# Single fp32 products in place of three rounded products of high and low parts

## What is computed

```python
def attention(h):                      # h: (8, 512, 256)
    q, k, v = heads(h @ W_q.T), heads(h @ W_k.T), heads(h @ W_v.T)
    p = softmax(causal(rope(q) @ rope(k).T / 4))
    return merge(p @ v) @ W_o.T

def ffn(h):                            # h: (4096, 256)
    cw = top4_of_top2_groups(sigmoid(h @ gate_w.T), gate_bias)
    y = sum(cw[:, e] * ((silu(h @ Wg[e].T) * (h @ Wu[e].T)) @ Wd[e].T) for e in range(16))
    return h + y + (silu(h @ Ws_g.T) * (h @ Ws_u.T)) @ Ws_d.T

x = x + ln(attention(ln(x)))
out = x + ln(ffn(ln(x)))
```

## Time and profile before

| what | value |
|---|---|
| time, median of 3 runs | 982.29 us (981.41 to 983.65) |
| profiled execution, span from first to last instruction | 1048.8 us (its time outside the span isn't listed) |
| mean granted clock of PE in it | 0.888 of full |
| busy share of the span: PE, PEld | 81%, 59% |
| busy share of the span: DVE, ACT, POOL | 62%, 44%, 41% |
| chain that ended last, by engine | PE 40%, DVE 23%, issue 11%, SPq 8%, DMA 6% |

### The profile page before, as it was taken

The page is one execution under the profiler, slowest core; times in us unless marked ns, Lnnn a source line. Parts: engine busy times, 40 slices in busy tenths (PEclk is TensorE's granted clock), DMA queues, the critical chain, the costliest instruction groups (busy, mean ns, idle before and its releaser), DMA issues.

```text
span 1048.8 us, 20609 instructions
## 1 busy us (share of the span) xinstructions
PE 852.6 (81%) x6580; PEld 615.2 (59%) x6580; DVE 652.3 (62%) x1914; ACT 456.3 (44%) x763; POOL 426.7 (41%) x408
## 2 busy tenths in 40 slices
PE   4569798987987987987987877978977799989955
PEld 3436374664664663664654545757865588867722
DVE  5577658687687687687586674533642233687916
ACT  2115454544544544544543555425433355544410
POOL 3222113135335335335213234374565555664621
PEclk9759898997897897997987998889999999998978
DMA  4685726236336336336395212453545566997783
GB/s 161 147 222 144 216 64 163 75 98 174 98 99 173 99 99 173 98 81 172 98 322 159 85 47 92 144 167 93 166 150 161 161 178 164 383 314 281 247 339 128
DMA packets 89175, 168.72 MB, mean 161 GB/s; under 512 B 14704, under 2 KB 56688, under 8 KB 88816
## 3 DMA queue, kind: packets, MB, share of 16 engines
q1 hardware_dynamic: 75248, 128.85, 42.1%
q0 software_dynamic: 13824, 38.55, 9.9%
HBM read 90.15 MB, written 76.68 MB: 159 GB/s over the span
## 4 chain that ended last, share of the span: by engine, by line
PE 40%; DVE 23%; issue 11%; SPq 8%; DMA 6%; another core or an unknown queue 5%; ACT 4%; POOL 3%; DVEq 0%; ACTq 0%; POOLq 0%
DVE nmax L829 8%; PE ring L1536 6%; PE ring L1314 5%; PE ring L1316 4%; PE ring L1315 4%; PE ring L1392 3%; PE ring L1557 3%; PE ring L1358 2%; SPq L628 2%; PE ring L1383 2%; SPq L629 2%; DMA xg<-sorted_rows 2%; PE ring L1436 2%; PE ring L1522 2%
## 5 line engine op out<-in xcount | busy, mean ns | idle before, releaser
L1244 ACT ACTIVATE prob<-ring 128x1024 f32<-128x1024 f32 (+1 forms) x192 | 167.5, 881 | 215.5 <-PE ring L1383 196.5
L829 DVE TENSOR_REDUCE nmax<-ring 128x2 f32<-128x1024 f32 (+3 forms) x256 | 201.8, 819 | 73.3 <-PE ring L1365 43.6
L736 POOL DMA_INDIRECT expert_rows<-ys,dest x160 | 159.2, 995 | 127.0 <-ACT ys L1198 74.8
L728 POOL DMA_INDIRECT sorted_rows<-xr,idx_all x128 | 130.5, 1019 | 104.8 <-DVE xr L991 71.5
L1536 PE MATMUL ring<-we,xh 128*128 x640 | 160.3, 396 | 0.0
L1536 PEld LDWEIGHTS ring<-we,xh 128*128 128x128 f32 x640 | 121.6, 200 | 14.6
L1054 DVE SCALAR_TENSOR_TENSOR sl<-sl,got,ring 128x128 f32<-128x128 f32 x160 | 48.3, 343 | 109.8 <-ACT sl L1296 62.5
L1358 PE MATMUL ring<-k_st,q_st 48*128 48x512 f32 (+3 forms) x512 | 88.9, 387 | 26.0 <-issue 9.7
L1392 PE MATMUL ring<-prob,v_sb 128*32 128x512 f32 (+3 forms) x1024 | 106.3, 518 | 3.2 <-ACT prob L1244 3.2
L1377 PE MATMUL ring<-maskt_b,halves_b 64*128 64x128 bf16 (+2 forms) x768 | 58.4, 233 | 50.7 <-DVE nmax L829 23.5
L1377 PEld LDWEIGHTS ring<-maskt_b,halves_b 64*128 64x128 bf16 x768 | 22.8, 97 | 125.4 <-issue 56.7
(11 more groups left out here) (203 smaller groups left out, 1650.8 us busy)
## 6 DMA issues: line engine op xcount, KB each, us to landing
xg<-sorted_rows SPq DMA_DIRECT2D x160, 134.0 KB
parts<-part SPq DMA_DIRECT2D x32, 512.0 KB
ykt<-expert_rows SPq DMA_DIRECT2D x14, 1024.0 KB
k_st<-parts SPq DMA_DIRECT2D x64, 128.0 KB
q_st<-parts SPq DMA_DIRECT2D x64, 128.0 KB
we<-w_exp SPq DMA_DIRECT2D x1, 6144.0 KB
sorted_rows<-zeros SPq DMA_DIRECT2D x2, 2144.0 KB, 9.6
sorted_rows<-zeros SPq DMA_DIRECT2D x32, 134.0 KB
```

The costliest lines, as they stand in the source:

```text
L728: pool.indirect_dma_start(out=xs[group_of(s)], out_offset=bass.IndirectOffsetOnAxis(ap=idx_all[:, s, t, k:k + 1], axis=0), in_=xr[:, s % 2 ...
L736: pool.indirect_dma_start(out=yk, out_offset=bass.IndirectOffsetOnAxis(ap=dest[:, j % 8, b:b + 1], axis=0), in_=ys[:, j % NYS, b, :], in_o ...
L829: dve.tensor_reduce(nmax[:, Q % 2, :, pp, qb], slot[:, :, col:col + (qb + 1) * P], AX.X, ALU.max, negate=True).then_inc(s_max, 1)
L1244: act_e.activation(prob[:, u % 2, 2 * half:2 * half + 2, 0:width], slot[:, :, 0:width], ACT.Exp, scale=SCALE).then_inc(s_exp, 1)
```

## The change

Every dense product becomes one matmul on fp32 tiles. ACT's copy out of PSUM stays (into `xt` and `h_t`); the low parts on DVE and POOL, the copy `a_hi`, the steps `GA`, the splits of the weights and the sum of the logit halves go. The weights are loaded straight into `wq` and `w_all`. What waited for a low part now waits for ACT's copy (`s_xt`, `s_at`, `s_ht`), for DVE's `act` (`SD`), or for the sigmoid (`M_BANK` after the logits). `act` is multiplied in place of its copy, so its next writer waits for the `SD` step of the sequence before. The logits have 16 columns. Nothing else of `PLAN` changes its place.

The diff, cut to its core:

```diff
-         ("GU", 0, 28), ("GU", 1, 28.01), ("GA", 0, 28.5), ("GA", 1, 28.9), ("LGA", 28.75), ("LG", 29.1)]
+         ("GU", 0, 28), ("GU", 1, 28.01), ("LGA", 28.75), ("LG", 29.1)]
...
-            "XT": lambda st: (s_xtlo, KD * (st[1] + 1)),
+            "XT": lambda st: (s_xt, KD * (st[1] + 1)),
...
-            "LGA": lambda st: (s_sumlg, st[1] + 1),
+            "LGA": lambda st: (s_score, st[1] + 1),
...
-            def xt_low(s, slot):
-                for k in range(KD):
-                    dve.wait_ge(s_xthi, KD * s + k + 1)
-                    dve.tensor_tensor(xt_lo[:, k, :], slot[:, k, :], xt_hi[:, k, :], ALU.subtract).then_inc(s_xtlo, 1)
...
                     if n:
-                        dve.wait_ge(s_alo, 2 * n - 1 + u)
+                        dve.wait_ge(s_sd, NHALF * n)
                     dve.tensor_tensor(act[:, u, :], silu[:, u, :], ring[RING_SLOT[st]][:, 1, :], ALU.mult).then_inc(s_t, 1)
-                elif kind == "LG":
-                    dve.wait_ge(s_logit, n + 1)
...
                 elif kind == "LG":
-                    act_e.wait_ge(s_sumlg, n + 1)
+                    act_e.wait_ge(s_logit, n + 1)
                     if n:
                         act_e.wait_ge(s_route, ROUTE_STEPS * n)
-                    act_e.activation(r_sc[:, :], r_lg[:, :], ACT.Sigmoid).then_inc(s_score, 1)
+                    act_e.activation(r_sc[:, :], M_BANK[:, 0:NT * E], ACT.Sigmoid).then_inc(s_score, 1)
...
-            def split_product(dst, l_hi, l_lo, r_hi, r_lo, start, stop, **kw):
-                pe.matmul(dst, l_lo, r_hi, start=start, stop=False, **kw)
-                pe.matmul(dst, l_hi, r_lo, start=False, stop=False, **kw)
-                return pe.matmul(dst, l_hi, r_hi, start=False, stop=stop, **kw)
...
                 for k in range(KD):
-                    last = split_product(slot[:, n, :], *weights(col, k, width, m, P), hi[:, k, :], lo[:, k, :],
-                                         k == 0, k == KD - 1)
+                    last = pe.matmul(slot[:, n, :], weights(col, k, width, m, P), rhs[:, k, :], start=k == 0, stop=k == KD - 1)
...
-                    dst = M_BANK[:, t * 2 * E:(t + 1) * 2 * E]
+                    dst = M_BANK[:, t * E:(t + 1) * E]
                     for k in range(KD):
-                        pe.matmul(dst, h_lo[:, k, tok], w_gate[:, k, :, :].rearrange("p c e -> p (c e)"), start=(k == 0), stop=False)
-                        last = pe.matmul(dst, h_hi[:, k, tok], w_gate[:, k, :, :].rearrange("p c e -> p (c e)"), start=False,
-                                         stop=k == KD - 1)
+                        last = pe.matmul(dst, h_t[:, k, tok], weights(C_GATE, k, E, 0, E), start=k == 0, stop=k == KD - 1)
```

More of the change, by code:

```diff
@@ L270, in block_kernel @@
         part = place("part", [P, 2, 2, T], fp32r)
[L271 to L274, removed]
+        xt = place("xt", [P, KD, T])
+        wq = place("wq", [P, C_O])
         rope_t = place("rope_t", [P, 2, T])
@@ L278, in block_kernel @@
         w_low = cursor[0]
[L279 to L284, removed]
+        w_all = place("w_all", [P, C_ALL - C_O])
+        h_t = place("h_t", [P, KD, T])
         pr = place("pr", [P, NT, D])
@@ L287, in block_kernel @@
         z = place("z", [P, NT, D])
-        a_hi = place("a_hi", [P, 2, T], fp32r)
-        a_lo = place("a_lo", [P, 2, T], fp32r)
+        w_high = cursor[0]
+        xr = place("xr", [P, 2, NT, XROW])
         silu = place("silu", [P, 2, T])
@@ L1116, in _ @@
                     norm_rows(n)
[L1117 to L1125, removed]
                 elif kind == "QK":
@@ L1202, in _ @@
                 slot = ring[RING_SLOT[st]] if st in RING_SLOT else None
-                if kind == "LX" and n == 0:
-                    act_e.wait_ge(s_wq, 16)
-                    copy(wq_hi[:, :], stage[:, 0:C_O], s_whi)
-                elif kind == "LNR" and n == 0:
-                    act_e.wait_ge(s_small, 16)
-                    copy(w_hi[:, :], stage[:, C_O:C_GATE], s_whi)
-                    copy(w_gate[:, :, 0, :], stage[:, C_GATE:].rearrange("p (k e) -> p k e", k=KD), s_whi)
-                elif kind == "XT":
+                if kind == "XT":
                     if n:
@@ L1278, in _ @@
                     act_e.activation(silu[:, u, :], slot[:, 0, :], ACT.Silu).then_inc(s_silu, 1)
-                elif kind == "GA":
-                    u = st[2]
-                    act_e.wait_ge(s_t, 2 * n + u + 1)
-                    if n:
-                        act_e.wait_ge(s_sd, NHALF * n)
-                    copy(a_hi[:, u, :], act[:, u, :], s_ahi)
                 elif kind == "BT1":
@@ L1340, in token_product @@
                     for k in range(KD):
-                        last = split_product(slot[:, t // 2, (t % 2) * D:(t % 2 + 1) * D], lhs_hi[:, k, tok], lhs_lo[:, k, tok],
-                                             *weights(col, k, width, m, D), k == 0, k == KD - 1)
+                        last = pe.matmul(slot[:, t // 2, (t % 2) * D:(t % 2 + 1) * D], lhs[:, k, tok],
+                                         weights(col, k, width, m, D), start=k == 0, stop=k == KD - 1)
                     if t % 2:
@@ L1494, in _ @@
                 elif kind in ("LGA", "LG"):
-                    pe.wait_ge(s_htlo, KD * (n + 1))
+                    pe.wait_ge(s_ht, KD * (n + 1))
                     logits_unit(n, int(kind == "LG"))
                 elif kind == "GU":
-                    pe.wait_ge(s_htlo, KD * (n + 1))
+                    pe.wait_ge(s_ht, KD * (n + 1))
                     for gu in range(2):
-                        channel_product(slot, gu, h_hi, h_lo, (C_SG, C_SU)[gu], D, st[2] * P, gu == 1).then_inc(s_gu, 1)
+                        channel_product(slot, gu, h_t, (C_SG, C_SU)[gu], D, st[2] * P).then_inc(s_gu, 1)
                 elif kind == "SD":
-                    pe.wait_ge(s_alo, 2 * n + 2)
-                    token_product(slot, a_hi, a_lo, C_SD, D, 0, s_sd)
+                    pe.wait_ge(s_t, 2 * n + 2)
+                    token_product(slot, act, C_SD, D, 0, s_sd)
                 elif kind == "CNT":
```

75 lines of the change are left out of this document (20 added, 55 removed).

## The result

| | before | after |
|---|---|---|
| time, median (lowest to highest), 4 runs each | 982.97 us (981.41 to 988.89) | 993.53 us (992.85 to 994.70) |
| span of the profiled execution | 1048.8 us, in a second execution 980.4 us | 989.9 us |

The ratio is 1.0097, interval 1.007 to 1.0125: 9.6 us more between the means, 10.6 between the medians.

The account below looks back on a forecast made before the run. Bound: PE's products and the waits for low parts, 336 to 389 us in a middle sequence. Costs of 4.5 less gains of 2.6 give 1.9 us, over 7.5 sequences 14 us: 996 us, 8 in 10 from 974 to 1020 us.

Parts of the forecast that it names:

- Products: On PE: single fp32 products 0.865 us at 512 columns, 0.433 at 256; 4.7 us more a sequence.
- What of it lies on the chain: Middle sequence, 336 to 389 us: 4.5 us of longer products on the chain; `OP`'s 0.6 us covered beside it.
- 0.4 us for the lower clock: Start of `GU` and half of `SD`: a product's excess is twice as long at the lower clock, 0.4 us more.
- What is given back: PE waits behind removed low parts in each sequence go: together 2.6 us.
- `h_lo`: Behind `HT` 0.85 us and ahead of `OP` 0.26 us of PE waits go in each sequence.
- `xt_lo`: At `XT`: PE's 0.64 us wait for a maximum that stands behind `xt_lo` goes.
- `a_hi` with the logit sum: Logits to sigmoid: PE's 0.85 us wait for `prob` goes.
- even start: First two sequences: products mostly at the lower clock; lost `xt_lo` gives back about what they cost more.
- piece without a name: Ahead of `HT`: unnamed 3.68 us stretch taken as unchanged; moving by 2 us a sequence equals the whole forecast.
- DVE's pace: Rival: DVE sets the pace and hides the products, so the change is faster, 968 us; chance 0.16.
- Nothing is given back: Rival: PE's waits for maxima move along with its later score units, 1020 to 1033 us; chance 0.12.
- The clock of a middle sequence: Rival: longer products keep PE at the upper clock over 349.9 to 356.6 us, 971 us; chance 0.05.

Follow-up runs that it names:

- e7: The kernel after with DVE again subtracting `h_lo`, and the slot and PE's products waiting for it: 999.23 us, ratio 1.016.
- e9: The kernel after with DVE again subtracting `xt_lo`, and the slot and first QK product waiting for it: 1001.73 us, ratio 1.0174.
- e10: The kernel after with `a_hi`, `a_lo` and a DVE pass over the logits ahead of the sigmoid put back: 1005.19 us, ratio 1.0224.
- e1: The kernel before, unchanged, profiled a second time: 982.27 us, span 980.4 us.
- e3: The kernel before with single fp32 products (logits as before), every low part still made and waited for: 1015.8 us, ratio 1.0318.
- e2: The kernel after with three rounded products each (two for the logits), a zero tile as low part, no low parts made: 968.97 us, ratio 0.9852.
- e5: The kernel after with V, SD and OP as three rounded products with a zero low part, QK and GU single: 985.31 us, ratio 1.0018.
- e6: The kernel after with QK and GU as three rounded products with a zero low part; V, SD and OP single: 975.62 us, ratio 0.9923.
- e4: The kernel after with one rounded matmul per product, less precise: 912.78 us, ratio 0.9273.
- e8: The kernel after with two rounded products per product, weights split in two parts, less precise: 940.14 us, ratio 0.9557.

## Why the prediction was right, and where only in the sum

- *Products.* Forecast starts of 0.865 and 0.433 us, measured 0.871 and 0.446; PE 35 us busier, measured 31.7. So the price of the earlier trace rows holds: each of the two records of a product takes about twice as long as a rounded one of its width (0.436 against 0.227 us at 512 columns), the product nearly four times as long. The Trainium skill, Perfetto Trace Analysis, Engine Utilization, halves the rate for FP32_LOW_HIGH; the trace agrees with that for a record, not for a whole product. The logits, taken as nothing, are nothing: four products in 1.00 us, eight rounded records before in 0.99 (337.65 to 338.64 us).
- *What of it lies on the chain.* 4.5 us a sequence (5.1 with `OP`). With the low parts still there it is 4.9 (73.4 to 78.3), of the 5.1 us that the measured starts make, so in sum almost nothing was covered. Without them it is 2.0 (71.8 to 73.8). The forecast took a price read in the trace of before, where it holds, and added it in the kernel after, where it doesn't. Its 0.4 us for the lower clock belong to the odd execution: in the second one the same place has a granted clock of 1.00 (the last but two of the numbers).

```profile
340.50:347.00 6.50, 4.52 (x55) 3.40 (x54) 5.51 (x20) 3.27 (x5) 4.80 (x6) 1.00 0.39 123
```

- *What is given back.* 2.6 us a sequence. With triples 1.6 come back (73.4 to 71.8), with single products 4.5 (78.3 to 73.8): `h_lo` 1.3 (forecast 0.85 + 0.26), `xt_lo` 1.0 (0.64), `a_hi` with the logit sum 2.0 (0.85). The last term is the one most mis-sized: PE's 0.85 us for `prob` came from the odd execution; in the second one the wait is 1.98 us in three of the four middle stretches. `h_lo` came near for another reason than the one given: the 1.08 us wait behind `HT` is not in the second execution, where PE waits only 0.27 us for `h_lo` in a middle stretch. In e7 it waits 0.5 us for `h_lo`, and 5.4 us ahead of the mask products where three of the four stretches after have 3.7: most of the term comes by the maxima, which follow on DVE. The other two go the way that was forecast: in e9 the wait ahead of `QK` is 0.6 to 0.8 us (after 0.2), in e10 that for `prob` 1.0 to 1.9 (after 0.4 or none). The rule "what counts is the PE wait behind each" gives 2.6 us where 1.6 come back if the products stay. It doesn't see that with longer products the low parts would hold up more, nor that what is left of the waits would then be used.
- *The sum.* 1.9 us a sequence were forecast, a middle sequence costs 0.4 (73.4 to 73.8). The 14 us came out as 9.7 because other places lost more than counted: 2.3 us up to the first mark, where products cost 7.9 to 8.0 and removals give 5.6 to 5.7 (forecast: even); 3.8 in the fifth stretch, 2.6 in the last. The reason given for the even start does not hold either: of the 216 rounded products that start there in the trace, only about 56 have the longer records of the lower clock (some 0.63 us at 512 and 0.41 us at 256 columns, in place of 0.39 and 0.28). So the sign was right, and the time came near in part by luck: the cost is not a loss of every sequence, a middle one loses a fifth of what was forecast, and places that the forecast did not single out made up for it. The 80.4 and 78.5 us of the forecast's signs belong to the odd execution, whose piece without a name is in no later one.
- *The fifth stretch.* The products cost there 4.6 (e1 to e3) to 5.0 us (e2 to after), the removals give 0.8 to 1.2. Its granted clock is 0.95 before and 0.90 after, and PE is busy 4.9 us longer, more than in a middle sequence. PE also waits longer for the row maxima that SP brings to `q_st`, just behind the load of the 6 MB of expert weights (503.7 to 524.7 us before, 510.1 to 529.9 after); timeline of PE, before, then after:

```profile
526.29 0.34 PE L1377 MATMUL ring<-maskt_b,halves_b 64*128 64x64 bf16 x4 [0.77 <-DMA q_st<-mrow]
```

```profile
533.88 0.34 PE L1297 MATMUL ring<-maskt_b,halves_b 64*128 64x64 bf16 x4 [2.32 <-DMA q_st<-mrow]
```

  The same wait is 2.2 us in e2 and e5 and 0.8 in e3, so it does not follow the products. The granted clock follows the loss better: e5 keeps 0.95 there and loses 1.4 us against e2, e6 has 0.88 and loses 3.1, e3 0.90. No run moved the load or held the clock; why this stretch loses more stays open.
- *Rivals.* DVE's pace holds in part, and only once the low parts are gone: it hides 2.7 of 4.7 us of a middle sequence, all of V, SD and OP. "Nothing is given back" is refuted by e2 and by the three single removals. The clock of a middle sequence is 0.92 to 0.95 before and 0.93 after, so it paid nothing there.

## What to carry to other kernels

A cost and a gain that touch the same idle time do not add up: size the cost in the kernel where the gain has already been taken, or run both halves alone. Where an edit trades work on a helper engine for longer work on the main one, look for the steps in which the longer work falls into a wait that stays; here that was `SD` and `OP`, and the wide products should have kept their parts. Before any term is read from a single profiled execution that is longer than the timed runs, profile it again.

## What the runs showed of the hardware

- The work behind the eighth mark, the same but for the last `SD`, took 289.9 to 303.8 us in thirteen executions, and a whole execution once 1048.8 in place of 980.4 us, with 318.8 us behind its last mark. Differences of a few us need marks, not spans.
- Shorter products went with a lower mean granted clock (shares of the upper level, 2.4 GHz): in the first two stretches behind the first mark 0.93 with three rounded products or one fp32 product and no low parts, 0.85 and 0.90 with one rounded product; over the span 0.888 for e4 and 0.893 for e8 against 0.917 for before.
- A matmul record of 16 columns on fp32 tiles costs as much as a rounded one of 32 columns: eight in 1.00 and 0.99 us.
